# Moving four of sixteen convolution taps from TensorE to VectorE, in an 8-core mixture-of-experts block

## The reference

```python
xn = _layernorm(x, axis=-1)                       # x: (8, 4096, 1024), D = 1024
# attention part: 21 taps, causal, one weight per tap and channel; tap 0 is zero
w = jnp.transpose(et)[:, None, ::-1]
h_hatt = jax.lax.conv_general_dilated(x_c, w, window_strides=(1,), padding=[(M - 1, 0)], ..., feature_group_count=Dn)
attn = xn @ W1 + h_hatt @ W2 + bias
# ffn part: a shared expert (2048 wide) and 16 routed experts (256 wide), 4 of 16 by sigmoid scores
shared_out = jax.nn.silu(sg) * su @ shared_down_w.T
h = jax.nn.silu(g) * u
hw = h * combine.T[:, :, None]
routed = jnp.einsum('esh,ehc->sc', hw, down_w)
x = x + attn + shared_out + routed
```

## Time and profile before

| | us |
|---|---|
| median of 2 runs | 3214.84 |
| the two runs | 3152.53 and 3277.15 |
| the profiled execution | 3156.02 |
| its span, slowest core | 3154.5 |
| its span, fastest core | 3131.1 |

### The profile page before, as it was taken

The page is one execution under the profiler, slowest core; times in us unless marked ns, Lnnn a source line. Parts: engine busy times, 40 slices in busy tenths (PEclk is TensorE's granted clock), DMA queues, the critical chain, the costliest instruction groups (busy, mean ns, idle before and its releaser), DMA issues.

```text
span 3154.5 us, 36591 instructions; the slowest of 8 cores (3131.1 to 3154.5 us)
## 1 busy us (share of the span) xinstructions
PE 2674.0 (85%) x11820; PEld 1152.8 (37%) x11820; DVE 1105.6 (35%) x2715; ACT 320.6 (10%) x580; POOL 599.7 (19%) x522
## 2 busy tenths in 40 slices
PE   2510179899989999899989999899989998999998
PEld 0200024344434444344434444344434443344443
DVE  5500013335332623334332623343342534253310
ACT  0000011100110011101110011001110011001100
POOL 0000123102320133112320133012310133002310
PEclk6755589999999999999999999999989999999999
DMA  8999964533354234643365235552455235532454
GB/s 120 132 125 119 109 119 147 175 122 96 117 181 149 54 124 146 175 116 99 121 185 143 61 121 157 167 111 87 138 179 150 61 118 176 146 82 87 147 154 127
DMA packets 85114, 405.29 MB, mean 128 GB/s; under 512 B 9650, under 2 KB 18098, under 8 KB 59074
## 3 DMA queue, kind: packets, MB, share of 16 engines
q1 hardware_dynamic: 65122, 319.05, 32.5%
q0 software_dynamic: 10592, 50.34, 13.6%
q10 hardware_dynamic: 9216, 33.56, 4.3%
HBM read 436.46 MB, written 58.72 MB: 157 GB/s over the span
## 4 chain that ended last, share of the span: by engine, by line
PE 77%; another core or an unknown queue 9%; DVE 6%; DMA 5%; issue 1%; ACT 0%; POOL 0%; DVEq 0%; POOLq 0%; ACTq 0%
PE ps L627 14%; PE ps L680 14%; PE ps L633 14%; PE ps L598 7%; PE ps L672 7%; PE ps L592 7%; PE ps L664 5%; PE ps L668 4%; DMA sh_sc<-shp 3%; DVE hcv L508 3%; DMA wdn<-dn_sc 2%; DVE diag L256 2%; PE ps L573 2%; PE ps L620 1%
## 5 line engine op out<-in xcount | busy, mean ns | idle before, releaser
L627 PE MATMUL ps<-xn_bf,wexp 128*128 128x512 bf16 x2048 | 485.1, 380 | 0.0
L633 PE MATMUL ps<-xn_bf,wexp 128*128 128x512 bf16 x2048 | 483.8, 379 | 0.0
L592 PE MATMUL ps<-xn_bf,wsh 128*128 128x512 bf16 x1024 | 251.9, 390 | 263.5 <-DMA wsh<-sh_sc 143.6
L680 PE MATMUL ps<-h_w,wdn 128*128 128x512 bf16 x2048 | 452.3, 379 | 9.6
L643 POOL TENSOR_TENSOR usb<-silu,usb 128x512 f32<-128x512 f32 x256 | 324.1, 1266 | 612.6 <-DVE usb L640 612.6
L646 DVE TENSOR_TENSOR h_w<-usb,ps 128x512 bf16<-128x512 f32 x256 | 176.0, 688 | 405.5 <-POOL usb L643 405.5
L605 DVE COPY usb<-ps 128x512 f32<-128x512 f32 x128 | 88.5, 692 | 612.0 <-PE ps L598 290.5
L680 PEld LDWEIGHTS ps<-h_w,wdn 128*128 128x128 bf16 x2048 | 195.7, 98 | 266.1 <-issue 39.3
L598 PE MATMUL ps<-xn_bf,wsh 128*128 128x512 bf16 x1024 | 256.4, 396 | 42.3 <-DVE h_conv L581 42.3
L633 PEld LDWEIGHTS ps<-xn_bf,wexp 128*128 128x128 bf16 x2048 | 200.4, 98 | 241.7
L627 PEld LDWEIGHTS ps<-xn_bf,wexp 128*128 128x128 bf16 x2048 | 189.8, 98 | 240.6 <-issue 29.0
(11 more groups left out here) (116 smaller groups left out, 1311.0 us busy)
## 6 DMA issues: line engine op xcount, KB each, us to landing
wexp<-ex_sc SPq DMA_DIRECT2D x128, 1024.0 KB, 5.6
wsh<-sh_sc SPq DMA_DIRECT2D x128, 512.0 KB, 3.9
wdn<-dn_sc SPq DMA_DIRECT2D x64, 1024.0 KB, 9.9
wdn<-dn_sc SPq DMA_DIRECT2D x64, 512.0 KB, 7.6
wdn<-dn_sc ACTq DMA_DIRECT2D x64, 512.0 KB, 5.0
ex_sc<-exp_p POOLq DMA_DIRECT2D x2, 8192.0 KB, 79.0
dn_sc<-dnp POOLq DMA_DIRECT2D x2, 8192.0 KB, 81.9
out_fm<-out_st SPq DMA_DIRECT2D x64, 256.0 KB, 3.3
```

The source lines that it names most:

```text
L592: [(lambda e, kc=kc, pg=pg, par_s=par_s, it=it: e.matmul(ps[pg][:], wsh[par_s][:, kc * 128:(kc + 1) * 128], xnbf_tok(it, kc), start=(kc == ...
L627: [(lambda e, kc=kc, hc=hc, pg=pg, par_e=par_e, it=it: e.matmul(ps[pg][:], wexp[par_e][:, kc * 256 + hc * 128: kc * 256 + hc * 128 + 128], ...
L633: [(lambda e, kc=kc, hc=hc, pu=pu, par_e=par_e, it=it: e.matmul(ps[pu][:], wexp[par_e][:, 2048 + kc * 256 + hc * 128: 2048 + kc * 256 + hc ...
L680: mmsb.append(lambda e, eh=eh, po=po, w0=w0: e.matmul(ps[po][:], w0[:, 4096 + eh * 128: 4096 + (eh + 1) * 128], h_w[:, eh * T:(eh + 1) * T ...
```

## The change

Four more taps (13 to 16) are computed on VectorE, so that TensorE makes taps 1 to 12 and VectorE taps 13 to 20. Fewer diagonal matrices are built. The call that loads the next tile's input stands behind the convolution's loop instead of ahead of it. Lines behind the moved call have the same numbers as before from L586 on; the convolution's matmuls are now L570 and the addition L578.

```diff
@@ -256,7 +256,7 @@
                      [(lambda e, j=j, kc=kc, par=par: e.tensor_scalar(
                          diag[par][:, (j - 1) * 128: j * 128], identbf[:],
                          et_sb[:, kc * 21 + j: kc * 21 + j + 1], None, ALU.mult))
-                      for j in range(1, 17)],
+                      for j in range(1, 13)],
                      reads=("identbf", "et_sb"), writes=(f"diag{par}",))
 
         def emit_x_load(i):
@@ -500,10 +500,10 @@
             hv = hcv2[kc % 2]
             bld.emit("vector",
                      lambda e, kc=kc, i=i, hv=hv: e.tensor_scalar(
-                         hv[:], xnbf_shift(i, kc, 17),
-                         et_sb[:, kc * 21 + 17: kc * 21 + 18], None, ALU.mult),
+                         hv[:], xnbf_shift(i, kc, 13),
+                         et_sb[:, kc * 21 + 13: kc * 21 + 14], None, ALU.mult),
                      reads=(f"xnbf{i % 2}_{kc}", "et_sb"), writes=(f"hcv{kc % 2}",))
-            for j in range(18, 21):
+            for j in range(14, 21):
                 bld.emit("vector",
                          lambda e, kc=kc, j=j, i=i, hv=hv: e.scalar_tensor_tensor(
                              hv[:], xnbf_shift(i, kc, j),
@@ -563,17 +563,14 @@
             if it == 0:
                 emit_tile_prologue(0)
 
-            if it + 1 < n_tiles:
-                emit_x_load(it + 1)
-
             for kc in range(KC):
                 par_d = kc % 4
                 pb = 2 + kc % 4
                 bld.emit("tensor",
                          [(lambda e, j=j, kc=kc, par_d=par_d, pb=pb, it=it: e.matmul(
                              ps[pb][:], diag[par_d][:, (j - 1) * 128: j * 128], xnbf_shift(it, kc, j),
-                             start=(j == 1), stop=(j == 16)))
-                          for j in range(1, 17)],
+                             start=(j == 1), stop=(j == 12)))
+                          for j in range(1, 13)],
                          reads=(f"diag{par_d}", f"xnbf{it % 2}_{kc}"), writes=(f"ps{pb}",))
                 if kc >= 2:
                     emit_conv_taps(it, kc)
@@ -583,6 +580,9 @@
                          reads=(f"ps{pb}", f"hcv{kc % 2}"), writes=("h_conv",))
                 if kc + 4 < KC:
                     emit_diag_build(kc + 4)
+            if it + 1 < n_tiles:
+                emit_x_load(it + 1)
+
             for hsc in range(16):
                 par_s = hsc % 3
                 sl = hsc % 2
```

## The result

The kernel is slower: the ratio of its time to that of the kernel before is 1.0324, with a 95% interval of 1.0309 to 1.0339. The executions compared take 3252 to 3256 us where those of before take 3151 to 3156 us; the profiled one took 3252.19 us, against 3156.02 us. In part of the executions of every kernel here some cores, pairs or a whole die, ran at a lower clock; these enter the medians over all executions (3443 us after, 3194 us before) but not the ratios, and where spans of an experiment are given for some cores, they are the ones without it.

A forecast was written before the change was run, and what follows sets the result against it. The prediction took VectorE's full list in the convolution stage, which TensorE waits for, as the bound. It summed 3156.0 us + 105.6 for the longer stage + 3 for the clock to 3265 us (+3.5%), range 3240 to 3315.

The forecast's parts named there:

- What bounds the kernel: Convolution: VectorE's list is full there without idle time and TensorE waits for it once per tile, 42.3 us in 8 waits.
- The stage: Convolution: additions 9.13 or 7.19 us apart, second L598 at T+55.3; 15.1 us longer a tile, 105.6 us over seven tiles.
- The clock term: New wait of 1.3 to 2.1 us ahead of the second L598 slows TensorE's clock; 3 us in all, ends 0 and 11.
- Taps at the tile's border hidden: End of the tile before: the 8 added taps of blocks 0 and 1, 6.9 us, fit VectorE's idle time, leaving 3.2 us.
- some 4 to 7 us: Sign to look for in the new profile: VectorE's idle time before the first addition drops to this.
- Tile 0: First tile: the convolution shifts by up to 22 us ahead of TensorE's 87.01 us wait for wsh; cost 0.
- The moved load: Load of x behind the convolution's loop: GpSimd's list stays the same, issued again 3 us after T; cost 0.
- The overlap of Vector instructions: VectorE's chained taps: if they overlapped by the skill's rule, 4 us a tile saved and about 3237 us.
- 1, time taken back at the output stage: Output stage: a later TensorE waits less for wdn, 61 us back, 3204 us; chance 4%.
- 2, TensorE sets the stage: Convolution: if tap spacing fell far below the trace's, 55 us of matmuls come off, 3101 us; chance 1%.
- 3, the clock falls more often: Groups behind the last wait run at the lower clock, some 4 us a tile, 28 us more, 3290 us; chance 10%.
- 4, the cover is gone: Stage start or tile 0: more than 3.2 us of VectorE's idle time lost, some 2 us a tile, 3279 us; chance 6%.

The follow-up runs named there:

- mid_only: Kernel before, with the four taps moved to VectorE only in blocks 2 to 7 and the load of x left ahead of the loop; ratio 1.0372.
- tail_only: Kernel before, with the four taps moved to VectorE only in blocks 0 and 1; no ratio, spans 3131 to 3134 us on cores 4 to 7.
- inter_after: Kernel after, with VectorE's taps of two blocks issued in turn; no ratio, spans 3210 and 3217 us on cores 2 and 3.
- t17: Made from the kernel after, with 17 taps on TensorE and 3 on VectorE; ratio 0.9949 (0.9896 to 1.0002).

## Why the prediction was right, point by point

- **What bounds the kernel: right.** VectorE's list in the convolution sets the second L598. mid_only (T+57.2) and tail_only (T+39.3) part the taps inside that list from those outside it.
- **The stage: right.** The first addition was to come at T+2.86 and came at T+2.87, the periods are 9.13 and 7.18 us for the 9.13 and 7.19 worked out. The second L598 was to start at T+55.3 and starts at T+55.5: 15.34 us a tile for 15.1, and 107.4 us for 105.6 (15.5 us a tile over all eight cores). Of the 0.2 us, 0.14 are the second addition's (T+5.60 for 5.46), and in some tiles, tile 3 among them, there is a gap of 0.47 us between two taps of the third block (9.50 us for 9.13), whose cause wasn't sought.
- **The clock term: right in kind, too large.** 3 us were taken from bounds of 0 and 11. The wait ahead of the second L598 was 1.66 us (1.3 to 2.1 forecast), and its eight matmuls took 1.89 us: full rate. The lower level was there in the 12.47 us wait's group and the L592 behind it (3.57 and 2.15 us), and in tile 3 in blocks 6 and 7 too (12 matmuls in 4.44 and 5.12 us on core 1), which the prediction's clock term didn't have; each time TensorE waits for VectorE again behind it, which hides it. On all eight cores the third L598 follows the second after 3.45 us in the mean, 16 matmuls at full rate, so the term is 0.
- **Taps at the tile's border hidden: right.** 5.01 us of idle time are left before tile 3's first addition on core 1, and 2.9 to 3.1 us before most others, in the new kernel and in tail_only. That is the 3.2 us worked out; the sign of "some 4 to 7 us" was set too high.
- **Tile 0: right.** Everything there shifts and still ends in the wait for wsh, which is over at the same time, 219.60 against 219.61 of the earlier trace rows. TensorE in the kernel after:

```profile
219.60 3.30 PE L592 MATMUL ps<-xn_bf,wsh 128*128 128x512 bf16 x8 [67.83 <-DMA wsh<-sh_sc]
```

- **The moved load: right so far as the trace shows.** L267 is issued at 1439.42, T+3.0, as forecast. mid_only, in which the load stays ahead of the loop, has all of the loss.
- **The sum.** 3265 us were forecast and 3252 measured, 0.4% apart. The 12 us between them are mainly the output stages, for which the forecast has no term: 133.5 us each before and 131.4 us after, on the two cores of the profiles. The rest nearly cancels (1.8 us more in the stage, 2.8 behind it, 3 us of clock term that didn't come, 1.7 us at the start of tile 1). The cores of one execution differ as much in their output stages (129.5 to 133.5 us before, 130.0 to 131.5 us after), and over all eight the mean goes from 131.8 to 130.9 us. The traces show what differs: the share of matmuls at the lower level. Two output stages of core 7 in the kernel after, 134.1 and 128.5 us long; the column ahead of the DMA share is the granted clock:

```profile
937.50:1071.60 134.10, 129.85 (x561) 55.79 (x562) 45.80 (x104) 10.42 (x24) 8.07 (x7) 0.94 0.36 113
1304.80:1433.30 128.50, 124.23 (x560) 54.32 (x561) 46.85 (x112) 10.43 (x24) 8.58 (x7) 0.99 0.40 120
```

  The waits inside the two are equal within 0.2 us. Over the 48 output stages of each profile, the matmuls more than 0.35 us apart lose 5.8 us a stage before and 5.1 after, and what is left of a stage is the same, 126.1 and 125.8 us. Why more of them fall into the lower level in one tile than in the next, and so whether the change has a part in it, is open.
- **The overlap of Vector instructions.** By the rule of the Trainium skill, "Perfetto Trace Analysis", Optimizing Scalar/DVE Operations, taken for chained taps, 3237 us would have come. The taps kept their 0.857 us and the rule doesn't hold for them; taps taken in turn (0.663 us apart, 0.75 long) do overlap, by 0.09 us. Two numbers of the prediction go wrong here. The 0.69 us that it put for the tap is the addition's duration, not its spacing (0.61); with the addition's overlap of 0.08 us a tap would take 0.67 us, 4.5 us a tile less, and the time would be 3233 us. And its lower bound rests on "a tap can't be spaced closer than its own 0.751 us": inter_after has them at 0.663. For the chained taps of this change the bound held.
- **Rivals.** 1, time taken back at the output stage: the wait for wdn is 72.1 us after 70.0, nothing is given back. 2, TensorE sets the stage: it is refuted, and t17 shows where it would begin. 3, the clock falls more often: it does, and the stretch's mean clock fell to 0.79, but the groups behind the last wait run at full rate, so it cost nothing. 4, the cover is gone: 2.9 to 5 us are left.

## What to carry to other kernels

An engine that is busy 35% of the span can still be full in the stage that counts: price a move by the list between the two events that bound that stage, and by the distance from one instruction's start to the next, not by a duration or a mean share. Of the same four taps those placed before a long idle time were a small gain (0.7 us a tile in tail_only) and those inside a full list cost 0.72 us each (mid_only: 17.2 us for 24). When an engine is late at a seam between stages, look at the order of buffers and chains too: letting the next stage begin in buffers that the last one didn't use, and taking two dependent chains in turn, gained 3.5 and 4.5 us a tile here without moving any work to another engine.

## What was not expected of the hardware

- A VectorE tap that reads the result of the one just ahead of it starts 0.194 us later than one that doesn't (0.857 and 0.663 us from start to start, at 128x512).
- A wait of TensorE of 1.66 us left the next eight matmuls at full rate (1.89 us), one of 5.63 us put them at 3.57 us and took 0.8 us more from the next eight. Between them the length of the wait doesn't settle it: ahead of block 6 in tile 3 of the kernel after all eight cores wait 2.26 or 2.27 us, and the 12 matmuls behind take 2.75 us on five cores and 4.4 us on three.
